# Storing x to the output rows ahead, halving the experts' rows, and letting the last scatter add

## The reference

```python
x = x + 0.5 * ffn(layernorm(x))       # called turn 0 below
x = x + attention(layernorm(x))       # 16 heads, causal, relative bias
x = x + 0.5 * ffn(layernorm(x))       # turn 1, same weights

def ffn(x):                           # x seen as (256, 16, 256)
    y1 = ln(x + mha(x)) * g1 + b1     # 4 heads over the 16 middle rows
    gates = softmax(y1 @ wg); idx = argmax(gates)     # 8 experts
    loc = position of the row among the rows of its expert
    keep = loc < 1024
    moe = where(keep, gate * ((y1 @ w1[idx] + b1[idx]) @ w2[idx] + b2[idx]), 0)
    return ln(y1 + moe) * g2 + b2
```

## Time and profile before

| | |
|---|---|
| median of 3 runs | 2509.3 us (2507.39 to 2509.95) |
| profiled execution, its own time | 2509.4 us |
| its span | 2507.7 us |
| turn 0: attention stage, from and to | about 21 to 436 us |
| turn 0: experts' stage | about 505 to 652 us |
| attention block in the middle | 657 to 1917 us |
| turn 1: attention stage | 1920 to 2339 us |
| turn 1: experts' stage | 2357 to the end |

### The profile page before, as it was taken

The page is one execution under the profiler, slowest core; times in us unless marked ns, Lnnn a source line. Parts: engine busy times, 40 slices in busy tenths (PEclk is TensorE's granted clock), DMA queues, the critical chain, the costliest instruction groups (busy, mean ns, idle before and its releaser), DMA issues. The chain is left out here.

```text
span 2507.7 us, 47389 instructions
## 1 busy us (share of the span) xinstructions
PE 2231.7 (89%) x15250; PEld 1330.2 (53%) x15252; DVE 1929.4 (77%) x5490; ACT 1569.3 (63%) x3207; POOL 919.2 (37%) x1158
## 2 busy tenths in 40 slices
PE   6999997977389889999999999999987999998474
PEld 4666666866155534444444444444465666666363
DVE  4677776589598788889888898998845677776496
ACT  2555554256144459999999999999941455554263
POOL 1577787036354400000000000000011387777166
PEclk7999998998699979999999999999998999999796
DMA  4233252856268424454444444444245122322673
GB/s 119 77 122 114 86 200 95 282 190 194 84 203 208 143 56 95 94 96 93 93 89 89 96 93 95 96 93 88 46 134 177 34 85 85 102 104 71 217 225 101
DMA packets 233752, 298.79 MB, mean 119 GB/s; under 512 B 43150, under 2 KB 181457, under 8 KB 232867
## 3 DMA queue, kind: packets, MB, share of 16 engines
q1 hardware_dynamic: 206483, 235.82, 36.8%
q0 software_dynamic: 17152, 50.49, 5.3%
q10 hardware_dynamic: 9872, 9.45, 1.2%
HBM read 203.36 MB, written 100.60 MB: 121 GB/s over the span
## 5 line engine op out<-in xcount | busy, mean ns | idle before, releaser
L2288 DVE CUSTOM_DVE_ANT_0 banks<-banks,ahead_bias 128x128 f32<-128x128 f32 (+7 forms) x1024 | 760.4, 776 | 94.1 <-PE banks L1997 80.5
L2203 ACT ACTIVATE attn_probT<-banks 128x512 f32<-128x512 f32 x1152 | 623.0, 608 | 72.3 <-PE banks L2014 61.8
L1997 PE MATMUL banks<-ahead_kst,ahead_qst 96*128 96x512 bf16 (+3 forms) x1536 | 425.9, 337 | 12.1 <-DVE attn_low L2288 7.4
L2014 PE MATMUL banks<-ahead_qst,ahead_kst 99*128 99x256 bf16 (+3 forms) x2176 | 394.9, 280 | 6.7 <-ACT banks L2194 1.3
L2345 POOL CAST attn_lowp<-attn_lowT 128x32 bf16<-128x32 f32 x64 | 13.4, 209 | 848.1 <-DVE attn_lowT L2296 848.1
L2036 PE MATMUL banks<-attn_probT,ahead_vb 128*32 128x256 f32 (+3 forms) x4352 | 315.6, 400 | 8.8 <-ACT attn_probT L2203 8.3
L2194 ACT COPY banks<-ahead_biasT 128x512 f32<-128x512 f32 x480 | 281.2, 611 | 16.3 <-PE banks L2052 6.6
L1997 PEld LDWEIGHTS banks<-ahead_kst,ahead_qst 96*128 96x128 bf16 x1536 | 118.9, 97 | 264.5 <-DVE attn_low L2288 174.3
L2014 PEld LDWEIGHTS banks<-ahead_qst,ahead_kst 99*128 99x128 bf16 x2176 | 180.8, 98 | 140.4 <-ACT attn_probT L2203 43.5
L438 PE MATMUL banks<-ffn_xT,winT 128*128 128x512 f32 x512 | 250.6, 613 | 4.6 <-DVE ffn_w L756 1.7
L977 POOL TENSOR_TENSOR ffn_w1T<-ffn_ring,own 128x512 f32<-128x512 f32 x128 | 134.4, 1062 | 176.5 <-PE banks L475 102.6
(11 more groups left out here) (259 smaller groups left out, 3955.3 us busy)
## 6 DMA issues: line engine op xcount, KB each, us to landing
ffn_ring<-disp SPq DMA_DIRECT2D x144, 257.0 KB, 3.2
ahead_qst<-qparts SPq DMA_DIRECT2D x384, 64.0 KB, 2.8
ahead_kst<-kparts SPq DMA_DIRECT2D x192, 128.0 KB, 5.0
ffn_ring<-in_L_attn_x_dram SPq DMA_DIRECT2D x32, 512.0 KB, 5.1
ffn_w<-in_L_ffn_w_dram SPq DMA_DIRECT2D x16, 1024.0 KB, 9.3
ahead_bias<-neard SPq DMA_DIRECT2D x128, 128.0 KB, 2.2
ahead_biasT<-neardT SPq DMA_DIRECT2D x128, 128.0 KB, 5.7
ffn_ring<-x SPq DMA_DIRECT2D x32, 512.0 KB, 4.9
```

Of the source, the lines that this page charges most:

```text
L1997: mm = nc.tensor.matmul(score[k % 2][:, a:e], qst[0:K6, u, half, hh, ii * P:(ii + 1) * P], kst[0:K6, u, hh, a:e], start=True, stop=True)
L2014: mm = nc.tensor.matmul(tbank[t % 3][:, at:at + nb * P], kst[:, u, hh, j * P:(j + 1) * P], qst[:, u, half, hh, x:x + nb * P], start=(k == ...
L2203: nc.scalar.activation(probT[:, g % 2, i, 0:w], tbank[t % 3][:, 0:w], ACT.Exp, scale=-1.0).then_inc(s_exp, 1)
L2288: nc.vector.tensor_tensor_reduce(out=part, in0=part, in1=bias[:, hh, T - w:T], scale=1.0, scalar=BIG, op0=ALU.add, op1=ALU.min, accum_out= ...
```

## The change

1. `ROW` becomes C + 2: y1, gate and number. The x rows have three buffers of their own, `xo`. SP loads x into them (`rows_x`), POOL adds ln2_b (`x_ahead`), and SP stores them to the output rows in order (`base_rows`). The ring's memory keeps its size (`room`), since the attention stage borrows it.
2. The last scatter becomes an accumulating indirect DMA (`compute_op=ALU.add`), behind a wait that the last x rows have landed (`based`). `scale` loses its second instruction.
3. SP writes the padding before it waits for `sent`.
4. `counted` also copies the counts to bf16 (`wholeb`), and `ranks` uses bf16 copies of the two matrices.
5. The root takes eps as its bias; L1513 goes.

```diff
-ROW = 2 * C + 2
+ROW = C + 2
 # ffn_attention, SP
         def rows_x(n):
-            slots_free(sp, n)
-            sp.dma_start(rb[:, n % 3, :, C:2 * C], xrow[:, n * GT:(n + 1) * GT, :]).then_inc(s_xl[n % 2], 16)
+            if n >= 3:
+                sp.wait_ge(s_xs[n % 3], n // 3 * 16)
+            sp.dma_start(xo[:, n % 3, :, :], xrow[:, n * GT:(n + 1) * GT, :]).then_inc(s_xl[n % 2], 16)
+        def base_rows(n):
+            sp.wait_ge(s_xb, n + 1)
+            sp.dma_start(outrow[:, n * GT:(n + 1) * GT, :], xo[:, n % 3, :, :]).then_inc(s_xs[n % 3], 16)
...
-            if n >= 3:
-                rows_x(n - 3)
+            if n >= 2:
+                rows_x(n - 2)
+            if n >= 4:
+                base_rows(n - 4)
...
 # PE
         def ranks(n):
             pe.wait_ge(s_rseed, n + 1)
-            pe.wait_ge(s_hot, n + 1)
-            pe.wait_ge(s_tally, 4 * n + 5)
+            pe.wait_ge(s_whole, n + 1)
-            nc.tensor.matmul(to, core.before[:, :], hot(n).rearrange("p t e -> p (t e)"), start=False, stop=False,
+            nc.tensor.matmul(to, beforeb[:, :], whole(n, 4, 8), start=False, stop=False,
                              skip_group_check=True)
...
 # DVE, end of counted(n)
+            dve.wait_ge(s_tally, 4 * n + 5)
+            if n >= 2:
+                dve.wait_ge(s_rank, n - 1)
+            nc.vector.tensor_copy(wholeb[:, n % 2, :, :], tally[:, n, :, :]).then_inc(s_whole, 1)
 # POOL
         def x_ahead(n):
             pool.wait_ge(s_xl[n % 2], n // 2 * 16 + 16)
-            xb = rb[:, n % 3, :, C:2 * C]
+            xb = xo[:, n % 3, :, :]
...
-                x_ahead(n - 1)
+            x_ahead(n)
 # ffn, SP
             sp.wait_ge(s_tot, 1)
-            sent(sp)
             for e in range(NE):
                 full = sp.value_load(toti[0:1, e:e + 1], min_val=0, max_val=S)
                 sp.dma_start(disp[bass.ds(full + e * REGION, P), :], pad[:, :]).then_inc(s_kept, 16)
...
+            sent(sp)
             sp.wait_ge(s_kept, 16 * NE)
 # POOL
             attend_gpsimd(pool)
+            based(pool)
...
-                    pool.indirect_dma_start(..., row(n, t, 0, C), None,
+                    pool.indirect_dma_start(..., row(n, t, 0, C), None, compute_op=ALU.add,
                                             bounds_check=S - 1, oob_is_err=False).then_inc(s_sent[n % RING], 16)
 # ACT
-                act.wait_ge(s_ve, n + 1)
-                nc.scalar.activation(ve[:, u, :], ve[:, u, :], ACT.Sqrt).then_inc(s_sd, 1)
+                act.wait_ge(s_mv, n + 1)
+                nc.scalar.activation(ve[:, u, :], mv[:, u, :, 1], ACT.Sqrt, bias=epsc[:, :], scale=1.0).then_inc(s_sd, 1)
 # DVE, experts' stage
-                nc.vector.tensor_scalar(ve[:, u, :], mv[:, u, :, 1], EPS, None, ALU.add).then_inc(s_ve, 1)
...
                 nc.vector.tensor_tensor(all_rows(n, 0, C), all_rows(n, 0, C), over(core.rows["ln2_g"][:, :], GT, 1),
-                                        ALU.mult).then_inc(s_scaled, 1)
-                dve.wait_ge(s_scaled, n + 1)
-                nc.vector.tensor_tensor(all_rows(n, 0, C), all_rows(n, 0, C), all_rows(n, C, 2 * C), ALU.add).then_inc(s_fin, 1)
+                                        ALU.mult).then_inc(s_fin, 1)
```

More of the change, by code:

```diff
@@ L289, in _, with ffn_attention @@
             nc.tensor.transpose(core.ps[:, 7, 0:NE * FB], b1raw[:, :], core.ident[0:NE * FB, 0:NE * FB]).then_inc(s_b1ps, 1)
-def ffn_attention(core, ph, lend, x, disp, s_disp, turn, route, tables, early_loads):
+def ffn_attention(core, ph, lend, x, out, disp, s_disp, turn, route, tables, early_loads):
     nc = core.nc
@@ L298, in ffn_attention @@
     xrow = x.rearrange("(p t) c -> p t c", p=P)
+    outrow = out.rearrange("(p t) c -> p t c", p=P)
     wide, kv, xs, spare = lend
@@ L302, in ffn_attention @@
     rb = wide.take(3, GT, ROW)
+    xo = wide.take(3, GT, C)
     xin = wide.take(4, GT, C)
@@ L320, in ffn_attention @@
     xT = xs.take(2, KB, GW)
-    tally, slot, number, eidx, ebase, zero = route
+    tally, wholeb, beforeb, onesb, slot, number, eidx, ebase, zero = route
     away, esum = wide.take(GT, NE), wide.take(GT)
@@ L325, in ffn_attention @@
     s_xb = ph.sem("xb")
+    s_xs = [ph.sem(f"xs{i}") for i in range(3)]
     (s_xst, s_xmv, s_xrs, s_xnb, s_xn, s_xTps, s_xTsb, s_qkps, s_qsb, s_ksb, s_vps, s_vsb) = (
@@ L353, in hot, with whole @@
         return tally[:, n, 4:8, :]
+    def whole(n, lo, hi):
+        return wholeb[:, n % 2, lo:hi, :].rearrange("p t e -> p (t e)")
     def exist(n):
@@ L385, in sync @@
         each(NG, body)
-        for n in range(NG - 3, NG):
+        for n in range(NG - 2, NG):
+            base_rows(n - 2)
             rows_x(n)
+        base_rows(NG - 2)
+        base_rows(NG - 1)
     def tensor(pe):
@@ L500, in ranks @@
             pe.wait_ge(s_rseed, n + 1)
-            pe.wait_ge(s_hot, n + 1)
-            pe.wait_ge(s_tally, 4 * n + 5)
+            pe.wait_ge(s_whole, n + 1)
             to = rank.rearrange("p t e -> p (t e)")
-            nc.tensor.matmul(to, core.before[:, :], hot(n).rearrange("p t e -> p (t e)"), start=False, stop=False,
+            nc.tensor.matmul(to, beforeb[:, :], whole(n, 4, 8), start=False, stop=False,
                              skip_group_check=True)
-            nc.tensor.matmul(to[:, 0:NE], core.ones[:, :], tally[:, n, 3, :], start=False, stop=True, skip_group_check=True)
-            nc.tensor.matmul(to[:, NE:GT * NE], core.ones[:, :], tally[:, n, 0:3, :].rearrange("p t e -> p (t e)"),
+            nc.tensor.matmul(to[:, 0:NE], onesb[:, :], whole(n, 3, 4), start=False, stop=True, skip_group_check=True)
+            nc.tensor.matmul(to[:, NE:GT * NE], onesb[:, :], whole(n, 0, 3),
                              start=False, stop=True, skip_group_check=True).then_inc(s_rank, 1)
@@ L638, in numbers @@
             slots_free(act, n)
-            nc.scalar.copy(rb[:, n % 3, :, 2 * C + 1:2 * C + 2], number[:, n * GT:(n + 1) * GT].unsqueeze(2)).then_inc(s_id, 1)
+            nc.scalar.copy(rb[:, n % 3, :, C + 1:C + 2], number[:, n * GT:(n + 1) * GT].unsqueeze(2)).then_inc(s_id, 1)
         if first:
@@ L1017, in sent, with based @@
             landed(eng, n)
+    def based(eng):
+        for n in range(NG - 3, NG):
+            eng.wait_ge(s_xs[n % 3], n // 3 * 16 + 16)
     def counted_all(eng):
@@ L1022, in counted_all @@
         eng.wait_ge(s_slot, NG)
-    return sync, tensor, scalar, vector, gpsimd, over_yet, sent, counted_all
+    return sync, tensor, scalar, vector, gpsimd, over_yet, sent, based, counted_all
 class Lent:
@@ L1048, in tile @@
             return ph.sb(n, [P, *shape], dt)
-        ring = tile("ring", RING, GT, ROW)
+        room = tile("room", RING * GT * (2 * C + 2))
+        ring = room[:, 0:RING * GT * ROW].rearrange("p (g t c) -> p g t c", g=RING, t=GT)
         tally, slot = tile("tally", NG + 1, 8, NE), tile("slot", TILES, dt=U32)
-        zero = tile("zero", 1)
+        wholeb = tile("wholeb", 2, 8, NE, dt=BF16)
+        beforeb, onesb = tile("beforeb", P, dt=BF16), tile("onesb", P, dt=BF16)
+        zero, epsc = tile("zero", 1), tile("epsc", 1)
         eidx, ebase, ei = tile("eidx", NE), tile("ebase", NE), tile("ei", NE, dt=I32)
@@ L1087, in ffn @@
         s_got = [ph.sem("got0"), ph.sem("got1")]
-        s_tps, s_tsb, s_zps, s_sum, s_st, s_mv, s_ve, s_sd, s_inv2, s_rs, s_norm, s_scaled, s_fin, s_marked, s_seed, s_inv, s_fac = (
-            ph.sem(x) for x in ("tps", "tsb", "zps", "sum", "st", "mv", "ve", "sd", "inv2", "rs", "norm", "scaled", "fin",
+        s_tps, s_tsb, s_zps, s_sum, s_st, s_mv, s_sd, s_inv2, s_rs, s_norm, s_fin, s_marked, s_seed, s_inv, s_fac = (
+            ph.sem(x) for x in ("tps", "tsb", "zps", "sum", "st", "mv", "sd", "inv2", "rs", "norm", "fin",
                                 "marked", "seed", "inv", "fac"))
@@ L1128, in load_w2 @@
             sp.dma_start(w2[:, e % 4, :, :], d["L0_ffn_w2"][e, :, :].rearrange("(k p) c -> p k c", p=P)).then_inc(s_w2[e % 4], 16)
-        lend = (Lent(ring[:, :, :, :].rearrange("p g t c -> p (g t c)")), Lent(w12[:, :, :].rearrange("p k c -> p (k c)")),
+        lend = (Lent(room[:, :]), Lent(w12[:, :, :].rearrange("p k c -> p (k c)")),
                 Lent(xT[:, :, :, :].rearrange("p u k c -> p (u k c)")),
                 Lent(w1T0[:, :, :].rearrange("p f c -> p (f c)")))
-        attend_sync, attend_tensor, attend_scalar, attend_vector, attend_gpsimd, over_yet, sent, counted_all = ffn_attention(
-            core, Phase(core, name + "_a", ph), lend, x, disp, s_disp, turn, (tally, slot, number, eidx, ebase, zero),
+        attend_sync, attend_tensor, attend_scalar, attend_vector, attend_gpsimd, over_yet, sent, based, counted_all = ffn_attention(
+            core, Phase(core, name + "_a", ph), lend, x, out, disp, s_disp, turn, (tally, wholeb, beforeb, onesb, slot, number, eidx, ebase, zero),
             tables, early_loads)
@@ L1192, in _ @@
                     i = n * GT + t
```

(5 more changed lines are left out.)

15 lines of the change are left out of this document (6 added, 9 removed).

## The result

The changed kernel took 2524.4 us (2521.4 to 2530.6, 5 runs) where the kernel before took 2509.95 (2507.4 to 2512.5, 5 runs): a ratio of 1.0062 (1.0044 to 1.0080), slower by 14 us. Forecast were 2466 us, in a range of 2452 to 2502. A second set of runs gave 1.0066 (1.0044 to 1.0088).

What follows compares the result with a forecast made beforehand. PE bounds attention and DVE the experts' stage, with POOL next. From 2509.4 us, 47.7 gained (29.2 + 2.6 + 7.5 + 8.4) and 4.5 lost (2.2 + 2 + 0.3) give 2466, range 2452 to 2502.

Steps and rivals of the forecast that it cites:

- the price of an accumulating scatter: Experts' stage, POOL: 1.00 us per scatter, between bounds of 0.96 and 1.97; 2.2 us lost over 144 scatters.
- Rival B2: Accumulating scatter costs POOL over 0.30 us above 1.00: slower than before, 2538 at 1.5, 2606 at 1.97; chance 0.10.
- B: Accumulating scatter's POOL time decides: 2481 to 2509 us at 1.1 to 1.3 (chance 0.17), slower beyond (0.10).
- POOL is late next: Experts' stage: POOL sets the pace at 5.63 us a group, 72 scatters start over 99.6; 14.6 us less per turn.
- The hold-up: Experts' stage: DVE's L1526 delays POOL's scatters by 0.47 us a group on the mean, 8.0 per turn.
- Rival D: Experts' stage: L1526 doesn't hold up POOL, or costs little; DVE's pace of 5.32 rules, 2455 us; chance 0.12.
- DVE's period of 5.32: Experts' stage: DVE's group falls from 6.65 to 5.32 us without scale's second instruction and L1513; PE, ACT, SP not late.
- The DMA engines: Experts' stage: accumulating scatters at twice the plain price, 4.5 us a group, hidden behind POOL's 5.63; later landing loses 2 us.
- Handover: Start of turn 1's experts' stage: padding starts 7.2 us sooner, with halved bytes; 7.5 us less, nothing in turn 0.
- Ranks: Attention stage, PE: bf16 matmuls save 0.3 us a group (bounds 0 and 0.59), 28 groups, 8.4 us less.
- x's own way: SP's loads and stores of x rows and POOL's bias add: costed at nothing; up to 1 us a group if stores delay loads.
- copies on DVE: Attention stage: bf16 copy of counts, 0.2 to 0.4 us, hidden, 0.3 lost once; two matrix casts 0.3 to 1 if not hidden.

Runs made afterwards that it cites:

- experiment 3: Changed kernel with last scatters of 64 of 128 rows, accumulating and plain: 2524.8 and 2503.6 us, against 2539.6 for the kernel before.
- experiment 4: Changed kernel with plain last scatters and DVE's product with ln2_g cut to 2 of 256 columns: 2515.2 us, ratio 0.9907.
- experiment 2: Kernel before with bf16 ranks alone: 2493.5 us; with early padding alone: 2505.7; with both and eps as the root's bias: 2481.7.

## Why the prediction was wrong

**The step that failed is the price of an accumulating scatter**: "I take a value near that row, 1.00", since it was "the same instruction with the same list". It is 1.55 in both runs of the changed kernel (medians of 1.551 to 1.554), so the term of 2.2 us should have been 0.57 x 144 = 82. Rival B2 is what happened, and its threshold, 0.30 above 1.00, was passed by 0.25. The argument used against B, that 514 and 256 floats cost alike, was about the bytes of a plain scatter and says nothing of another form; experiment 3 shows that what grows is the call, by 0.42, and the rows, by 0.15. With 0.96 and 1.97 as bounds, the middle (1.46) would have been nearer than the plain row beside it. The estimate that the prediction drew from the Trainium skill's sentence on reductions in the DMA engines (Collectives: The Full Stack, section "The bandwidth ceiling: the fold count and why AG ≠ RS ≠ AR") was 1.5 times. The trace has 1.58 times on POOL, but 3 times the packets and 3.0 to 3.2 times the DMA engines' time, so it agrees in direction and nearly in size on POOL only.

**POOL is late next**: right. Without the add it came to 99.9 and 101.7 us for 99.6. The hold-up of 8.0 us per turn was in truth 5.3 there ((1.059 - 0.985) x 72), and DVE's waits made up the rest; in the changed kernel it was 2.7 ((1.590 - 1.552) x 72), since POOL's starts are further apart. Rival D's mechanism, no hold-up, is refuted by experiment 4: the Trainium skill's rule that a tensor_tensor leaves descriptor generation alone (SBUF — State Buffer, section "Who interferes with whom"), which the page calls inferred, doesn't hold for these scatters, 0.985 us beside a 2-column product and up to 1.93 beside the whole one.

**DVE's period of 5.32**: nearly. With plain scatters its groups are 5.16 and 5.7 us apart. But what I had not listed is the loop of PE, DVE and ACT, 5.4 us a group at full clock, a bound just under POOL's 5.63. It took 6.3 at the lower clock, and 7.6 where DVE's product was cut.

**The DMA engines**: the price of an accumulating scatter was taken at twice the plain one, 0.64, and is 1.02. A group needs 4 x 1.02 + 4 x 0.49 = 6.0 of the 7.6 us that POOL takes (134.9 / 71 x 4): hidden, as forecast, but only because POOL was slower too, for 6.0 is more than the 5.63 of the forecast.

**Handover**: 7.2 us for 7.5, though experiment 2 shows that it depends on the halved rows (by the order alone 2.6 to the first fetch). **Ranks**: 0.51 a group for 0.3, 15 us for 8.4. **x's own way** at nothing, the **copies on DVE** hidden (0.20 for `wholeb`): right.

Put right one by one, the forecast comes out: 2466, plus 82 - 2 for the scatters, less 6.5 for ranks, less 11 for the hold-up (2 x (8.0 - 2.7)), is 2529, against 2524.

## What to carry to other kernels

An operation moved from an engine into a DMA is paid by the engine that issues it, too: before letting an indirect DMA accumulate, count the calls and take a measured duration of that form, not that of its plain neighbour. Where no row shows a price and the whole gain divided by the count (here 0.30 us) is smaller than the distance between the bounds, the forecast should stand between them, and a test of that one instruction comes first. Making the busiest engine lighter can cost time: here 26 us, with the engines behind it in a longer loop. Read from the chain what stands in that loop, and don't put its length down to the clock before a run at the other level shows it.

## What the runs showed of the hardware

- An accumulating indirect DMA of 128 rows of 1 KB takes 1.55 us of POOL against 0.985 plain (1.40 against 0.907 for 64 rows), about 139 packets against 48, and 1.02 us of the 16 DMA engines against 0.32 to 0.34.
- A DVE tensor_tensor of 128x1024 f32 lengthens a scatter that starts inside it, by up to 1.05 us; sums from PSUM and statistics on DVE don't (144 scatters beside them took 0.982 to 0.996 us).
- Three small bf16 matmuls (32, 8 and 24 columns) give the next product after 0.08 us; in f32 it was 0.59.
- The last of eight padding writes of 257 KB landed in 5.75 us beside scatters (4.6 to 5.3 in three other runs), in 2.65 alone; at 129 KB in 3.04 beside them (2.9 to 3.7 in others).
- The loop of PE, DVE and ACT took 10.8 us for two groups with 16 products in 3.73 us and 12.5 with them in 5.42. With DVE's product cut it took 15.3, at a granted clock of 0.83, and the same 15.3 with the products at 3.72 us.
- The kernel before differed by 1.2% between chips (2508 and 2540 us), all of it outside the experts' stage; with plain scatters and rows of 258 floats 35 of 41 us lay inside it.
